# New homes for the first experts' tiles, and B and C of the state-space layer read from two row groups

## What is computed

```python
for L in range(4):
    h = layernorm(x) * (1 + ca) + sa
    x = x + ga * attn[L](h)
    h = layernorm(x) * (1 + cb) + sb
    x = x + gb * ffn[L](h)
```

```python
# L0 ffn: two rounds, each a shared and two routed experts (8 experts of 64)
for _ in range(2):
    ctx = concat([integrated, v])                 # 256 wide
    ctrl = gelu(ctx @ w1[e] + b1[e]) @ w2[e] + b2[e]
    alpha, beta, gate = sigmoid, softplus, sigmoid of the thirds of ctrl
    v_next = alpha * v - beta * (x - mu); x_next = x + 0.1 * gate * v_next
    ...                                           # halt and refine
# L1 attn: 8 heads, blocks of 32 tokens
qp = elu(q @ proj[h]) + 1; kp = elu(k @ proj[h]) + 1
out = (qp @ (kp.T @ v)) / (qp @ sum(kp))
# L3 attn: a state-space scan with 16 states, over all tokens in order
dt = softplus(x @ Wdt + bdt); B = x @ WB + bB; C = x @ WC + bC
h[t] = exp(dt[t] * A) * h[t-1] + x_ssm[t] * dt[t] * B[t]
y[t] = sum over the 16 states of h[t] * C[t]
# L3 ffn: top 2 of 8 experts, 128 -> 512 -> 128, weights gathered by row
```

## Time and profile before

| what | value |
|---|---|
| median of 3 runs | 1316.84 us (1313.4 to 1318.43) |
| the profiled execution, its own time | 1318.67 us |
| its span, first to last instruction | 1316.6 us |
| PE busy | 1153.3 us (88%) |
| DVE busy | 860.4 us (65%) |
| ACT busy | 700.3 us (53%) |
| POOL busy | 495.6 us (38%) |
| mean granted TensorE clock | 0.903 |

### The profile page before, as it was taken

One profiled execution on the slowest core, in us unless ns is written; L12 is line 12 of the kernel. 1 busy time (PEld: TensorE's weight loads), 2 busy tenths in 40 slices (PEclk: granted clock), 3 DMA queues, 4 the chain that ended last, 5 costly groups with the idle time before them and its releaser, 6 DMA issues.

```text
span 1316.6 us, 15319 instructions
## 1 busy us (share of the span) xinstructions
PE 1153.3 (88%) x5374; PEld 732.3 (56%) x5374; DVE 860.4 (65%) x2005; ACT 700.3 (53%) x1166; POOL 495.6 (38%) x482
## 2 busy tenths in 40 slices
PE   7998899998999999999999989789696978969583
PEld 6775443333434466655676444455345856858583
DVE  3756446456364457668888999988985888935131
ACT  3557564766657667653355762626363866633110
POOL 2212312223121101013434356463655767583532
PEclk9999899899998968998799988858887988989787
DMA  8400000000000000000000000000004644658573
GB/s 269 172 1 0 1 0 0 1 1 0 1 0 1 0 1 1 1 16 17 1 1 1 16 1 0 16 1 1 1 0 143 220 161 143 216 172 264 191 229 102
DMA packets 41820, 77.82 MB, mean 59 GB/s; under 512 B 3344, under 2 KB 30992, under 8 KB 41232
## 3 DMA queue, kind: packets, MB, share of 16 engines
q0 software_dynamic: 10688, 51.39, 11.7%
q1 hardware_dynamic: 31056, 25.46, 6.1%
HBM read 65.83 MB, written 11.01 MB: 58 GB/s over the span
## 4 chain that ended last, share of the span: by engine, by line
PE 57%; DVE 15%; ACT 8%; issue 7%; POOL 6%; DMA 5%; another core or an unknown queue 1%; SPq 0%; POOLq 0%; DVEq 0%; ACTq 0%
PE ps L876 7%; PE ps L2082 5%; PE ps L1447 3%; PE ps L2090 3%; PE ps L1265 3%; PE ps L838 2%; DMA own<-sx 2%; PE ps L649 2%; PE ps L1274 2%; PE ps L1567 2%; PE ps L1562 2%; PE ps L663 1%; PE ps L1721 1%; DVE own L1641 1%; PE ps L1909 1%
## 5 line engine op out<-in xcount | busy, mean ns | idle before, releaser
L876 PE MATMUL ps<-own,g_f 128*128 128x512 f32 x320 | 143.3, 600 | 5.2 <-DVE own L1084 5.2
L1204 POOL TENSOR_TENSOR own<-own 128x512 f32<-128x512 f32 x32 | 38.7, 1209 | 176.2 <-PE ps L876 105.5
L876 PEld LDWEIGHTS ps<-own,g_f 128*128 128x128 f32 x320 | 60.5, 192 | 78.6 <-issue 66.2
L2182 DVE TENSOR_TENSOR own<-ps,own 128x512 f32<-128x512 f32 x60 | 41.1, 685 | 85.9 <-PE ps L2082 48.6
L2005 DVE TENSOR_TENSOR_SCAN own<-own,carry 128x512 f32<-128x512 f32 x48 | 79.6, 1661 | 19.2 <-POOL own L2029 12.7
L2116 ACT ACTIVATE own<-ps 128x512 f32<-128x512 f32 x60 | 35.5, 596 | 96.3 <-PE ps L2082 70.0
L2082 PE MATMUL ps<-own,g_l 128*128 128x128 f32 x480 | 66.1, 291 | 9.4 <-DMA g_l<-w,slot 3.3
L504 POOL TENSOR_SCALAR sm<-sm 128x4 f32<-128x4 f32 x32 | 9.5, 296 | 171.0 <-DVE sm L496 170.1
L1084 DVE TENSOR_TENSOR own<-own 128x512 f32<-128x512 f32 x32 | 23.4, 732 | 73.5 <-PE ps L876 67.0
L2082 PEld LDWEIGHTS ps<-own,g_l 128*128 128x128 f32 x480 | 62.0, 205 | 16.5 <-issue 7.4
L1865 POOL TENSOR_TENSOR own<-own 128x512 f32<-128x512 f32 x32 | 42.2, 1318 | 64.8 <-DVE own L1839 41.3
(11 more groups left out here) (416 smaller groups left out, 3140.8 us busy)
## 6 DMA issues: line engine op xcount, KB each, us to landing
sx<-brow SPq DMA_DIRECT2D x4, 960.0 KB, 11.4
own<-sx SPq DMA_DIRECT2D x12, 256.0 KB, 5.8
so<-own SPq DMA_DIRECT2D x12, 256.0 KB
g_l<-p_l SPq DMA_DIRECT2D x1, 2449.0 KB, 12.9
g_f<-p_f SPq DMA_DIRECT2D x1, 2223.5 KB, 9.2
own<-cs SPq DMA_DIRECT2D x8, 256.0 KB, 3.0
g_l<-p_l SPq DMA_DIRECT2D x1, 1866.0 KB, 7.5
g_l<-t_wmod SPq DMA_DIRECT2D x1, 1152.0 KB, 9.8
```

What stands on the lines that cost most here:

```text
L876: x = e.matmul(s.bank["V%d%d%d" % (it, k, cc)][:, :], ew2[:, m, 128 * cc:128 * cc + 128], gm, start=False, stop=m == 3)
```

## The change

`ORDER` is another string; with it nearly every row of every engine stands elsewhere. The code changes in these places.

- `Room`: chunks 0 and 1 use the tiles of chunks 2 and 3 as before, and `early[0:2]` or a new buffer `spare`. Chunks 2 and 3 use `early` and `g_a` in place of tiles of chunks 0 and 1. `room_clear` holds the new waits: chunk 2 begins behind L0A of all chunks and L0F of chunk 0; chunk 3 begins behind L0F of chunks 1 and 2. L1A of chunks 0 and 1 waits for no other chunk's L0F.
- L1A: six feature tiles instead of seven; the second pair of q and k projections is written over the first, in the tiles `T[c][0]` and `T[c][10]`, and so comes behind the maps of head 3.
- L3A: the split into three bf16 parts is made before the transpose, on 128 columns (four tokens' groups of 32 values) for each DVE instruction, and ACT casts the transposed 128 rows to bf16. B of a state lies in 24 rows from row 0 or 32, C in 24 rows from row 64 or 96. `sel` (128 by 8, made once) picks a state. B and C matmuls of a state are issued together.
- L3F: chunks 0, 1 and 2 use ring 0, chunk 3 ring 1. Chunk 0's first fetch waits for the end of all L0F instead of all L1A.

```diff
 ORDER = (
-    "ytytyojkokopekplppfmolaoqlnqafoqnfaonmsqqsogmrasrfefssrirrheooeobobagooaagbobgkobgkkjaaolbbobbbobdkdcoiceihkydkkfofhjdk"
+    "ytytyojkkoopekplpppfmoolaqqmaofororfnaqqlamqnfnarfaaraasrhsekkkkkkkgsksksioeoeofofkcbohdocbgahcogibaoffiddhgaiaaokjabkkf"
...
             def __init__(self, c):
-                t, o = T[c], T[c ^ 2][2:11]
-                z = [early[:, (4 * (c % 2) + i) * W:(4 * (c % 2) + i + 1) * W] for i in range(4)]
+                e = [early[:, i * W:(i + 1) * W] for i in range(8)]
+                t, o = T[c], T[c + 2][2:11] if c < 2 else e + [G["a0"][:, :]]
+                z = [b[:, :] for b in spare] if c else e[0:2]
...
+        def room_clear(q, c):
+            if c < 2:
+                q.wait_ge(*ST[0][c + 2].dve("x"))
+            elif c == 2:
+                for k in range(NC):
+                    q.wait_ge(*ST[0][k].dve("x"))
+                q.wait_ge(*ST[1][0].dve("x"))
+            else:
+                q.wait_ge(*ST[1][1].dve("x"))
+                q.wait_ge(*ST[1][2].dve("x"))
...
             q.wait_ge(landed["f0"], 16)
             q.wait_ge(*s.act("h"))
-            q.wait_ge(*ST[0][s.c ^ 2].dve("x"))
-            if s.c >= 2:
-                q.wait_ge(*ST[1][s.c ^ 2].dve("x"))
+            room_clear(q, s.c)
...
             q.wait_ge(landed["proj"], 128)
-            if c < 2:
-                q.wait_ge(*ST[1][c + 2].dve("x"))
...
-            for n in range(4):
-                yield
+
+            def project(n):
                 p = banks.take(s, q, "qk%d" % n, (s.act, "qk%d" % n))
...
                 if hd < 8 and hd % 2 == 0:
                     yield
                     yield from maps(hd)
+                if hd == 2:
+                    for n in (2, 3):
+                        yield
+                        project(n)
...
             for n in range(19):
                 if n < 16:
+                    j, a = n // 2, 32 * (n % 2)
                     yield
                     p = banks.take(s, q, "B%d" % n, (s.act if n % 2 else s.dve, "B%d" % n))
-                    e.matmul(p[:, :], threeb[:, n:n + 1].broadcast_to([96, 128]), bc3, start=True, stop=True).then_inc(*s.pe.up("B%d" % n))
-                    yield
+                    e.matmul(p[:, :], sel[a:a + 24, j:j + 1].broadcast_to([24, 128]), bc3[a:a + 24, :], start=True, stop=True).then_inc(*s.pe.up("B%d" % n))
+                    a += 64
                     p = banks.take(s, q, "C%d" % n, (s.dve, "C%d" % n))
-                    e.matmul(p[:, :], threeb[:, 16 + n:17 + n].broadcast_to([96, 128]), bc3, start=True, stop=True).then_inc(*s.pe.up("C%d" % n))
+                    e.matmul(p[:, :], sel[a:a + 24, j:j + 1].broadcast_to([24, 128]), bc3[a:a + 24, :], start=True, stop=True).then_inc(*s.pe.up("C%d" % n))
...
             q.wait_ge(*s.dve.now())
-            e.tensor_copy(tile4(T[c][2])[:, :, 0:96].rearrange("p t (r n) -> p t r n", n=32), bc.unsqueeze(2).broadcast_to([128, 4, 3, 32])).then_inc(*s.dve.up("X"))
+            e.tensor_copy(hi, b8).then_inc(*s.dve.up("hi"))
+            yield
+            q.wait_ge(*s.dve.now())
+            e.tensor_tensor(b8, b8, hi, ALU.subtract).then_inc(*s.dve.up("rest"))
+            e.tensor_copy(X[:, :, 2:4, :], hi.unsqueeze(2).broadcast_to([128, 16, 2, 8])).then_inc(*s.dve.up("X2"))
+            yield
+            q.wait_ge(*s.dve("rest"))
+            e.tensor_copy(mid, b8).then_inc(*s.dve.up("mid"))
+            yield
+            q.wait_ge(*s.dve.now())
+            e.tensor_tensor(X[:, :, 0, :], b8, mid, ALU.subtract).then_inc(*s.dve.up("X0"))
+            e.tensor_copy(X[:, :, 1, :], mid).then_inc(*s.dve.up("X"))
...
-            yield
-            q.wait_ge(*s.act("XT"))
-            yield from split_vector(s, q, e, T[c][3].bitcast(BF16)[:, 0:W], T[c][2])
...
         def weights3(c, j):
-            b = ring3[c % 2][(c // 2 * NJ + j) % 4]
+            b = ring3[c // 3][(c % 3 * NJ + j) % 4]
```

174 lines of the change are left out of this document (93 added, 81 removed).

## The result

The changed kernel takes **1310.06 us** (median of 14 runs, 1292.51 to 1315.37), the kernel before in the same session 1317.51 (14 runs, 1312.09 to 1322.24). The ratio is 0.9923, 95% interval 0.9894 to 0.9951: 0.8% faster, where 2.3% were forecast. Three runs of the changed kernel (1313.06, 1314.58 and 1315.37 us) lie over 1.5% above its fastest, count as slow and are left out of the ratio; the two medians of all runs alone would give 0.6%. The runs spread more widely than before: one of the 14 took 1292.51 us, 11.7 us less than the next, and its trace was not kept. The profiled execution is one of the quicker ones, 1304.17 us, at a granted clock of 0.906, where the median over the 14 runs is 0.8975.

What follows compares the result with a forecast made beforehand. PE, busy 88%, was taken as first bound, held by many small waits where DVE is overloaded, plus clock loss. 1318.7 - 4 - 4 - 25 + 2 = 1287.7, less 1.8 for the median, gave 1286 us; range 1256 to 1313.

Steps and rivals of the forecast that it cites:

- the order's 25 us: L0F's room and the order: DVE work leaves 840 to 1030 us, PE stands less; 25 us less, bounds 0 and 50.
- the mixed stretch: Where L0F runs beside other stages: PE's 9% standing in 700 to 840 us, taken as measure for 840 to 1200.
- B and C in row groups: L3A's 64 pairs at 0.37 us instead of 0.43: 4 us less of PE, bounds 14 less to 4 more.
- The rule on changing tiling modes: Skill page: changing tiling mode drains TensorE; at both ends of L3A's pairs, 0.49 us each, 4 us more instead of less.
- The early split: L3A's split ahead of the transpose: DVE gets 7 us back, a little over half counted, 4 us less, bounds 0 and 8.
- Homes, rings and order: Room and order 25 us less; L1A's late projections 2 us more; L3F's rings counted as nothing.
- Chunk 3 comes late: Rival: chunk 3's L0F ends near 635 us, its six steps take 700 instead of 650; 1337 us, chance 10%.
- The pile forms again: Rival: PE stands for DVE's interleaved L2A, L1A and L3A as in 840 to 1030; 1311 us or nothing, chance 10%.
- the small terms: What the pile's case keeps without the order's 25 us: row groups, split and late projections, 6 us less together.
- The clock decides more: Rival: L1A's small matmuls mixed with L0F's full ones raise the mean clock from 0.90 to 0.93; 1268 us, chance 15%.
- The sum: All terms taken from the profiled execution, 1318.7 - 4 - 4 - 25 + 2 = 1287.7 us, forecast as a 1286 us median.
- What was to be seen: Signs: pairs starting together, PE busy 5 us less, PE standing at most 12%, DVE 60%, chunk 3's L0F ending 610 to 660.

Runs made afterwards that it cites:

- full-row series: Changed kernel with B and C picked from all 128 rows, one behind the other, order and everything else kept: 1292.61 us, ratio 0.9816 to the kernel before.
- without carries: Changed kernel with chunk 3's scans in L2A and L3A started from zero, not waiting for chunk 2's carries: 1309.47 us, ratio 0.9939.
- the old order: Kernel before, its order and rooms kept, with the new L3A: 1322.14 us with 53 of 64 pairs side by side, 1321.02 us with full rows.
- old L3A: Changed kernel with its rooms, rings and order, but L3A's split and its B and C as before (96 rows): 1306.95 us, ratio 0.9922.

## Why row groups cost time here

Four kernels vary how the pairs run. First the number of rows, then running at once, each alone:

```diff
-                    e.matmul(p[:, :], selw[:, w:w + 1].broadcast_to([128, 128]), bc3, start=True, stop=True).then_inc(*s.pe.up("B%d" % n))
+                    e.matmul(p[:, :], selw[0:64, w:w + 1].broadcast_to([64, 128]), bc3[0:64, :], start=True, stop=True).then_inc(*s.pe.up("B%d" % n))
```

This is B of the half-row kernel; C has rows 64 to 127. The kernel with the same rows for both drops one line of the changed kernel, so that C reads B's row group and runs behind it:

```diff
-                    a += 64
```

> The changed kernel with B picked by a 64-row selector from rows 0 to 63 and C by one from rows 64 to 127 (zeros outside the row that is picked), so that the pair still runs side by side, but over all 128 rows. The question is why the 24-row pairs cost 17 us against the full-row series (1292.6 us, granted clock .912 to .918, against about 1310 us and .890 to .906). Theory Rows (what counts is how many of TensorE's rows a matmul keeps busy, through the granted clock): near the full-row series, 1286 to 1297 us, clock at or above .91. Theory Side by side (two matmuls at once in row groups, or the step into them, is what costs): near the changed kernel, 1305 to 1313 us, clock below .905. Theory Pattern (any small shift of the order changes the time by up to 15 us either way, rows have nothing to do with it): anything from 1290 to 1312, with no relation between it and the run with 24 rows in series.

> The changed kernel with C's matmul reading the same 24 rows and the same selector rows as B's (so C's values are B's and the third attention's output is not the reference's): the two of a pair share a row group, and run one after the other. Theory Rows: the few rows stay, so the time stays at 1303 to 1315 us and the clock below .905. Theory Side by side: the cost goes, 1290 to 1298 us, clock at or above .91. Theory Pattern: no relation to the half-row run.

Measured: half rows 1307.5 us (1300.83 to 1311.37), ratio 0.9916 [0.9890, 0.9943]; same rows 1299.94 us (1296.2 to 1301.01), ratio 0.9860 [0.9838, 0.9882]. Using all 128 rows doesn't help as long as the pair runs at once, so the theory of rows falls as the whole cause. In series with 24 rows 10 of the 17.5 us are back (8 of 14 by the ratios); that lies between Rows (1303 or more) and Side by side (1298 or less), so neither theory has it whole. This kernel is not the plain series either: its two matmuls keep the step from the whole array to the row group and back, and in the trace a pair costs 0.63 us from start to start, 0.21 more than at once.

Then the changed kernel with one full matmul more ahead of each pair:

```diff
+                    e.matmul(p[:, :], selw[:, 0:1].broadcast_to([128, 128]), bc3, start=True, stop=True)
```

> The changed kernel, its 24-row pairs side by side as they are, with one more matmul ahead of each pair: a full 128-row one of the same 512 columns into B's bank, whose values the pair's B then overwrites (64 matmuls of some 0.22 us, 14 us more PE work, nothing computed differently). Theory Activity (what the pairs cost is granted clock: TensorE does less in the same time, and the half-clock stretches, of which the longest of the changed kernel runs from 766.8 to 835.1 us, grow): the filler gives the clock back, .905 or more, and in spite of 14 us more work the time is 1295 to 1308 us, at or below the changed kernel's 1310. Theory Mixing (the step between whole-array and row-group matmuls costs each time, whatever the clock): the same steps and 14 us more, 1318 to 1326 us. Theory Path (the fill is simply work on the path that sets the end): 1320 to 1324 us with the clock unchanged at about .897.

Measured: 1305.19 us (1297.82 to 1311.86), ratio 0.9908 [0.9874, 0.9942]; the median clock over its runs is 0.9075, against 0.8975 of the changed kernel. Some 14 us of useless work on the busiest engine cost nothing that can be measured. Mixing and Path, which wanted 1318 us or more, are both refuted.

Where the difference arises can be read directly, since the changed kernel and the full-row one have the same order on every engine. Set side by side instruction by instruction, the changed kernel's PE is 0.8 us behind at 634 us, where the pairs of chunk 0 begin, 1.1 at 748 and at 766, 8.8 at 784, 16.2 at 814 and 16.8 at 829; from there on it wins 6 us back, and is 10.6 behind at 1271. No pair of B and C runs in it between 744 and 815 us. So the cost falls on other matmuls than the pairs, while over the pairs of chunk 0 themselves the two kernels keep step. The windows of the changed kernel:

```profile
752.00:766.00 14.00, 12.31 (x67) 8.03 (x64) 11.52 (x22) 8.42 (x19) 9.99 (x10) 0.88 0.01 2
766.80:783.90 17.10, 17.10 (x62) 12.06 (x66) 10.29 (x20) 7.81 (x16) 4.92 (x8) 0.50 0.00 0
787.30:835.10 47.80, 42.75 (x167) 32.53 (x166) 28.65 (x75) 19.01 (x36) 11.78 (x12) 0.50 0.00 1
```

and of the full-row kernel:

```profile
751.70:766.00 14.30, 12.69 (x74) 9.09 (x76) 11.93 (x25) 7.71 (x17) 10.29 (x11) 0.88 0.00 1
766.00:779.60 13.60, 13.19 (x96) 9.91 (x88) 12.84 (x35) 10.68 (x21) 5.77 (x7) 1.00 0.00 1
779.60:789.90 10.30, 10.30 (x45) 9.27 (x45) 5.64 (x11) 2.44 (x7) 2.54 (x2) 0.50 0.00 0
789.90:800.10 10.20, 9.94 (x80) 7.63 (x79) 7.90 (x16) 4.92 (x9) 3.80 (x3) 1.00 0.01 2
800.10:817.20 17.10, 12.71 (x37) 7.57 (x37) 14.87 (x44) 10.63 (x20) 5.46 (x7) 0.50 0.00 0
```

Up to 766 the rows are alike. Then PE comes to the small matmuls of chunk 2's L1A. The changed kernel is granted half clock (1.2 GHz) for 17.1 and 47.8 us; in the first of these PE is busy 17.10 us of 17.10, so nothing waits, everything is slow. The full-row kernel begins the same instructions at full clock and has half clock for 10.3 and 17.1 us of them. Over the spans the clock loss is 0.094 x 1301.9 = 122.4 and 0.085 x 1288.8 = 109.5 us: 12.9 of the 13.1 us between the two spans.

A row of the Trainium skill (TensorE: Matmul & The Clock Gate, "Why this matters for your kernels") lays a drop in mid-kernel to idle gaps between bursts of matmuls. Here the row of 766.80 shows half clock with no gap in it, and the 14 us ahead of it have as much idle time in the changed kernel (1.7 us) as in the full-row one (1.6), so gaps don't tell the two apart.

**Is it the 16 pairs just ahead?** The pairs of chunk 0 run from 634 to 744 us; the other 48 come from 815 on.

```diff
+                    if c == 0:
+                        e.matmul(p[:, :], selw[:, w:w + 1].broadcast_to([128, 128]), bc3, start=True, stop=True).then_inc(*s.pe.up("B%d" % n))
+                    else:
+                        e.matmul(p[:, :], sel[a:a + 24, j:j + 1].broadcast_to([24, 128]), bc3[a:a + 24, :], start=True, stop=True).then_inc(*s.pe.up("B%d" % n))
```

The second kernel has `c > 0` in its place; C goes likewise.

> The changed kernel with B and C of chunk 0 picked from all 128 rows in series (16 of the 64 pairs, which run from 634 to 744 us), and those of chunks 1 to 3 in row groups side by side as they are. In all traces so far that hold one, the half-clock stretch from 767 to 835 us stands right behind chunk 0's third attention, and it makes up all of the 16 us between the changed kernel and the full-row one. Theory Local (chunk 0's pairs decide whether that stretch comes): 1290 to 1299 us. Theory Spread (each pair costs its 64th, wherever it stands): 1303 to 1308 us, three quarters of the cost remaining.

> The reverse: chunk 0's 16 pairs side by side, the 48 of chunks 1 to 3 picked from all 128 rows in series. Theory Local: the stretch comes as in the changed kernel, 1303 to 1312 us. Theory Spread: 1294 to 1300 us.

Measured: full rows in chunk 0 alone **1294.25 us** (1290.52 to 1296.61), ratio 0.9801 [0.9780, 0.9823]; full rows in chunks 1 to 3 alone 1300.86 us (1299.89 to 1306.33), ratio 0.9871 [0.9849, 0.9892]. The windows of the first,

```profile
766.00:784.30 18.30, 17.89 (x129) 14.02 (x129) 17.38 (x45) 13.53 (x28) 8.34 (x9) 1.00 0.00 1
784.30:794.50 10.20, 10.20 (x44) 9.17 (x44) 5.67 (x11) 2.46 (x7) 2.54 (x2) 0.51 0.00 0
```

and of the second:

```profile
771.20:788.30 17.10, 17.10 (x63) 12.06 (x66) 10.34 (x21) 7.73 (x16) 4.95 (x8) 0.50 0.00 0
791.60:825.70 34.10, 33.88 (x146) 28.30 (x147) 15.51 (x35) 11.32 (x21) 6.58 (x6) 0.50 0.00 1
```

The first kernel gets 129 matmuls through in 18.3 us, the second 63 in 17.1. (The first pays a little of it ahead: its clock is 0.61 from 753 to 766 us, where the changed kernel's is 0.88.) Whether the long stretch comes is decided here by chunk 0's 16 pairs: undoing these alone returns 15.8 of 17.5 us, as Local said. But the second kernel came out between the theories (Local wanted 1303 or more): it keeps the stretch and is 9 us faster all the same (7 by the ratios). That its stretch ends earlier is not the reason. Side by side, the distance between it and the changed kernel stays at 4.5 us from 250 to 910 us, this stretch included; it wins 6 us between 910 and 1100 us, among the later pairs. (The two profiled spans are 1298.1 and 1301.9 us.) The two gains add up to more than the whole, so the costs are not independent.

The long stretch tells the kernels apart better than the mean clock. Among the kernels that differ from the changed one in B and C or the carries alone, it stands in the profile of every one whose chunk 0 pairs run at once without filler: the changed kernel, half rows, without carries, chunks 1 to 3 full. It stands in none of the others: full rows, chunk 0 full, 24 rows in series, with filler. Each is one profile. That speaks against Pattern as the whole answer, but no run makes a neutral shift ahead of 766 us in the new order, the old order shows no effect at all, and the one run of the changed kernel at 1292.51 us shows that it can take the full-row kernel's time without any edit. The granted clock alone does not fix the time either: the profiled executions with filler, with 24 rows in series and with chunks 1 to 3 full lose 120.5, 122.0 and 122.0 us to the clock by (1 - clock) x span, as much as the changed kernel's 122.4, and are 4 to 7 us shorter; they lose it in other places.

The median granted clock over all runs of a kernel follows the times only roughly: full rows 0.916 (1292.61 us), chunk 0 full 0.913 (1294.25), old L3A 0.9085 (1306.95), with the filler 0.9075 (1305.19), 24 rows in series 0.907 (1299.94), chunks 1 to 3 full 0.905 (1300.86), half rows 0.9005 (1307.5), the changed kernel 0.8975 (1310.06), without carries 0.894 (1309.47). What in the matmuls ahead makes the chip grant the lower level stays open. The kernels without the stretch have one thing in common: in chunk 0 each pair's matmuls run one behind the other, or a third, full one runs ahead of them; in those with it the two share the time of one. Why 128 rows in series are 7 us faster than 24 is not explained by this.

## Where the order's 25 us went

POOL's sum of two products left out, in the kernel after and before (PE adds one product of each two; half the states are missing):

```diff
-                    q.wait_ge(*s.pool("sum%d" % k))
+                    q.wait_ge(*s.dve("C%d" % (2 * k + 1)))
...
-                    e.tensor_tensor(a, a, T[c][AH[(2 * k + 1) % 4]], ALU.add).then_inc(*s.pool.up("sum%d" % k))
```

> The changed kernel without GpSimd's sums of the products of two states in the third attention (32 of 512 columns by 128 rows), PE adding one product of each two instead (half the states are left out of y). In the changed kernel PE stands 20.4 us for these sums, in the kernel before for VectorE's work ahead. Theory A (the new order moved the wait from VectorE to GpSimd, and that is where the rest of the forecast 25 us went): 12 to 22 us faster than the changed kernel, and clearly more than the same edit gives in the kernel before. Theory B (GpSimd's sum is only the last link, VectorE's products come as late): at most 6 us from 1310.

> The same edit in the kernel before: its sums of two products left out, half the states missing from y. Theory A: 0 to 6 us faster than 1317.5. Theory B: the same gain or none in both kernels, within 4 us of each other.

Measured: 1281.26 us (ratio 0.9727 [0.9692, 0.9761]) after and 1299.04 us (0.9849 [0.9812, 0.9887]) before: by the ratios 1.96% or 25.8 us less than the changed kernel, and 1.51% or 19.9 us less than the kernel before. The difference of 6 us is not to be told from none, with intervals of some 6 us either way on the first gain and 5 on the second. The first gain is more than A's 22 and the second far more than its 6; B's 6 us is refuted. POOL's sums held both kernels alike, and with more than PE's waits for them (14.0 us before, 20.4 after). Part of both gains is the clock: by (1 - clock) x span of the profiled executions 10 us after and 12 before.

DVE's scans over 256 of 512 columns:

```diff
-                    e.tensor_tensor_scan(H, A, H, init, ALU.mult, ALU.add).then_inc(*s.dve.up("H%d" % n))
+                    e.tensor_tensor_scan(H[:, 0:256], A[:, 0:256], H[:, 0:256], init, ALU.mult, ALU.add).then_inc(*s.dve.up("H%d" % n))
```

> The changed kernel with VectorE's scans of the third attention over the first 256 of 512 columns (the rest of each state row is left unscanned; the output is not the reference's). VectorE's work falls by some 35 us, spread over four chunks. In the kernel before VectorE's pile held PE at L2090 (15.5 us) and L1909 (14.0 us). Theory A (the new order spread VectorE's pile, and the wait is GpSimd's now): 3 to 12 us faster than 1310, and less than the same edit gives in the kernel before. Theory B (VectorE still holds the middle stretch, GpSimd's sums only follow its scans): 15 us faster or more, and as much as in the kernel before.

> The same edit in the kernel before. Theory A: 12 to 25 us faster than 1318, more than it gives in the changed kernel. Theory B: within 4 us of what it gives there.

Measured: 1276.03 us (0.9662 [0.9615, 0.9709]) after, 1305.83 us (0.9887 [0.9832, 0.9942]) before, by the ratios 2.61% or 34 us against 1.13% or 15 us. DVE is busy 36.3 us less in the first (829.4) and 34.0 less in the second (826.4), so a microsecond of the scans gave back one in the new order, and about half of one before. Neither theory has both numbers: A wanted the smaller gain in the changed kernel, B the same in both. And most of the difference between the orders is the clock again, not DVE's place on the path. By (1 - clock) x span the profiled execution after the edit loses 108.4 us instead of 122.4, 14 less, and the stretch at 767 us is gone although its pairs run at once (in the kernel after without POOL's sums too); the one before loses 130.3 instead of 127.7. The two spans are 26.7 us (1301.9 to 1275.2) and 13.4 us (1316.6 to 1303.2) shorter; without the clock that leaves 13 us of gain after and 16 before, for 36.3 and 34.0 us of work. So these runs show that DVE's scans hold both orders, each microsecond with 0.3 to 0.5 besides the clock; they don't show that the new order put DVE on the path or took it off. Where the rest of the forecast 25 us went stays open.

## Why the prediction missed, point by point

Two terms carry the miss. The row groups were sized as PE's own time alone, with no term for the clock of what follows; and the order's 25 us rested on PE standing only 9% in the mixed stretch. The split erred the other way and hid part of it.

- **B and C in row groups, forecast -4, measured +17.5 (+14 by the ratios).** The term's own working held. In 50 of the 64 pairs the two start within 0.01 us of each other (in the other 14 C starts 0.03 to 2.8 us behind B). A lone pair costs 0.41 us from start to start against 0.43 in series: 0.10 to step into row groups, 0.21, and 0.10 to step back. Two pairs that stand next to each other use four row groups and run all at once, 0.42 us for 0.86. Some 7 such doubles and 50 single pairs give 4 us, an estimate from these figures and the size forecast. What failed is the step that made busy time into time. The bounds of -14 to +4 came from the pair's own duration; the pairs' effect on the clock of what follows them had no term, and it is 12.9 us between the two profiled executions. The rule on changing tiling modes was weighed as a cost at each pair; measured at both ends it is 0.2 us a pair, which is inside the bounds, and not the reason: the cost lies where no pair runs.
- **The early split, -4, measured -14.3 in the new order and nothing in the old.** I counted a little over half of 7 us of DVE's time. In the new order (1 - clock) x span gives 9.2 us of the step (118.7 to 109.5), and PE's idle time is 8.6 us shorter (170.4 to 161.8). The forecast had no term for the clock here either. Whether the split or the step from 96 to 128 rows brought the clock back is not separated.
- **Homes, rings and order, -25 and +2, measured -10.3.** The step that failed is "what PE loses where the load is mixed": I let 840 to 1200 fall to 9% standing, and from 840 to 1185 it still stands 16%. Nor did I count that the mixed stretch gets holes of its own (510 to 700, 4% to 12%), the longest behind POOL and ACT: from 605 to 770 us PE waits 6.3 us for L3A's sums, 3.9 for L2A's additions and 6.2 at L544. That chunk 0's L3A, moved forward, holds PE there is in line with these waits; no run shows it alone.
- **The rivals.** *Chunk 3 comes late*: its L0F ended at 604.2 us rather than 635, and its six steps took 694 us instead of 650; the two errors leave 13 us. Without the carries nothing changes, so these don't hold it. *The pile forms again* is closest in the number (1311 forecast, 1310 measured) and in part in the cause: PE's idle time did stay. But the agreement of the number is luck: it left the small terms at -6, where the split gave 14 us, the row groups took as much or more, and the order still gave 10. *The clock decides more* named a mechanism that counts, for another reason (small matmuls mixed with full ones, which no run tests) and with a far larger gain: by (1 - clock) x span the order gave 9 us, the split as much, and the row groups took 13 back, so 5 are left between the profiled executions.
- **The sum.** Its arithmetic holds. One reading is a little off: DVE's slices show 8 and 9 from slice 19 on, not 17; nothing is worked out from it.
- **What was to be seen.** Right: the next matmul 0.32 us behind a pair, PE's busy time, the last chunk's tiles (1227.26 to 1281.67, 54.4 us), DVE beside chunk 3's L0F (76%). Right for 50 pairs of 64: the common start. Wrong by a little: PE stands 12.9% from 596 to 993, and chunk 3's L0F ends 6 us too early. The sign of being wrong that came true is the last one: PE's idle time has only gone to other stretches. The three fences are windows of the changed kernel, the source line that ends L0F, and PE's timeline at the two ends of the last chunk's tiles.

```profile
430.00:604.00 174.00, 169.26 (x649) 90.73 (x647) 131.76 (x289) 102.15 (x163) 57.56 (x55) 0.97 0.01 4
596.00:993.00 397.00, 345.93 (x1597) 223.88 (x1595) 313.60 (x656) 199.71 (x362) 179.42 (x163) 0.83 0.11 38
```

```profile
L1209 DVE TENSOR_TENSOR xs<-ps,xs x4: 691/691/692, 226.6 to 603.5; 128x512 f32<-128x512 f32 x4
```

```profile
1227.26 3.74 PE L2118 MATMUL ps<-own,g_l 128*128 128x128 f32 x32
...
1279.49 2.18 PE L2126 MATMUL ps<-g_l,own 128*128 128x128 f32 x16
```


## What to carry to other kernels

When a change makes TensorE work less in a stretch, look at the granted clock of the stretches behind it before believing the saved microseconds: here the same instructions ran at half clock 23 us behind the last pair of chunk 0. Packing two matmuls into row groups is worth trying against the plain full-row version, not only against what stood there before; here the plain version of the same change is the fastest kernel that computes everything, 1292.61 us, together with the one that has full rows in chunk 0 alone (1294.25). To learn whether an engine is on the path, shorten its work in both orders, and take the clock out of both gains before comparing: here spans shorter by 26.7 and 13.4 us looked like a path that had moved, and the 13 and 16 us besides the clock do not.

## What was not expected of the hardware

VectorE's scans take longer when GpSimd adds beside them. By their source line (ns, min/median/max) the scans of the changed kernel take 1.28 us in the median, but up to 3.49:

```profile
L2041 DVE TENSOR_TENSOR_SCAN own<-own,carry x48: 1269/1283/3493, 825.1 to 1172.7; 128x512 f32<-128x512 f32 x48
```

POOL's timeline and DVE's show the longest one:

```profile
1070.94 1.28 POOL L2065 TENSOR_TENSOR own<-own 128x512 f32<-128x512 f32 x1
1072.16 1.28 POOL L2071 TENSOR_TENSOR own<-own 128x512 f32<-128x512 f32 x1
1073.39 1.27 POOL L1258 TENSOR_TENSOR xs<-xs,g_l 128x512 f32<-128x512 f32 x1
...
1072.26 3.49 DVE L2041 TENSOR_TENSOR_SCAN own<-own,carry 128x512 f32<-128x512 f32 x1 [1.50 <-POOL own L2065]
```

The scan starts 0.1 us behind a POOL addition and ends 1.1 us behind the end of the next one (1074.66), as if it had stood until then. With POOL's sums left out the same scans are shorter (groups of instructions, busy us and mean ns; first the changed kernel, then without the sums):

```profile
L2041 DVE TENSOR_TENSOR_SCAN own<-own,carry 128x512 f32<-128x512 f32 x48 | 72.4, 1508 | 19.6 <-POOL own L2065 13.3 <-ACT own L1972 5.2 <-ACT carry L1983 0.9
```

```profile
L2041 DVE TENSOR_TENSOR_SCAN own<-own,carry 128x512 f32<-128x512 f32 x48 | 64.6, 1345 | 20.6 <-POOL own L2065 12.9 <-ACT own L1972 4.8 <-ACT carry L1983 2.8
```

The Trainium skill has a rule that fits (SBUF — State Buffer, "SBUF: two separate sides"): a VectorE instruction with two inputs in SBUF and a GpSimd instruction that reads SBUF share one pair of ports, which the first holds to its end, while the other blocks. The scan reads two tiles of SBUF and the addition too. The trace agrees, with 1508 against 1345 ns for the mean scan. It may be a part of why POOL's sums cost more than PE's waits for them; no run takes it apart.
